# Loading the gated feed-forward's first operands during the last batch of lane attention

## The reference, cut to what matters

```python
x = x + tanh(g_xattn[1]) * L1_xattn(layernorm(x), ctx, ctx, ...)   # "lane attention"
x = x + tanh(g_ffn[1]) * L1_ffn(layernorm(x), gate_w, up_w, down_w, gate_a, ...)

def _L1_ffn_ref(x, gate_w, up_w, down_w, gate_a, gate_b, up_a, up_b, down_a, down_b):
    gate = _matmul_lora(x, gate_w, gate_a, gate_b)      # x @ w.T + (x @ a.T) @ b.T
    up = _matmul_lora(x, up_w, up_a, up_b)
    hidden = jax.nn.silu(gate) * up
    return _matmul_lora(hidden, down_w, down_a, down_b)
```

## Time and profile before

| what | us |
|---|---|
| median of 3 runs (lowest, highest) | 3406.77 (3404.89, 3408.68) |
| the profiled execution's own time | 3397.87 |
| its span, first to last instruction | 3396.2 |
| PE busy in the span | 3206.3 (94%) |
| last matmul of lane attention starts | 1878.14 |
| first matmul of the gated feed-forward starts | 1893.09 |
| its first product (L2329) starts | 1910.27 |

### The profile page before, as it was taken

How to read it: one execution, slowest core, us unless ns; L and a number is a source line. 1 busy time by engine, 2 the same in 40 slices (tenths; PEclk the granted TensorE clock), 3 DMA queues, 4 the chain that set the end, 5 groups by cost and what they waited for, 6 DMA issues and landing times. The chain is left out here.

```text
span 3396.2 us, 52096 instructions
## 1 busy us (share of the span) xinstructions
PE 3206.3 (94%) x20924; PEld 2468.6 (73%) x20924; DVE 1424.9 (42%) x2020; ACT 893.4 (26%) x1233; POOL 347.8 (10%) x304
## 2 busy tenths in 40 slices
PE   7999569998999989999999799999999999999999
PEld 4656437777788866666666688888888888778777
DVE  8888588882200028787777321222212122300000
ACT  3333343332211125555454211111111111200000
POOL 2000000000000013332232101111110100000000
PEclk9999779998999989999999799999999999999999
DMA  6776522212422231221221432222222222642443
GB/s 144 154 153 133 173 76 72 75 63 87 143 66 63 74 130 69 82 99 74 80 80 56 164 114 95 100 88 101 88 95 95 99 94 104 228 152 96 145 143 104
DMA packets 341895, 361.09 MB, mean 106 GB/s; under 512 B 154624, under 2 KB 261744, under 8 KB 339840
## 3 DMA queue, kind: packets, MB, share of 16 engines
q1 hardware_dynamic: 338304, 356.28, 33.2%
q10 hardware_dynamic: 3456, 2.90, 0.3%
HBM read 215.23 MB, written 135.36 MB: 103 GB/s over the span
## 5 line engine op out<-in xcount | busy, mean ns | idle before, releaser
L2329 PE MATMUL g_ps<-g_xs,g_wt 128*128 128x512 f32 x4128 | 948.9, 390 | 0.0
L2329 PEld LDWEIGHTS g_ps<-g_xs,g_wt 128*128 128x128 f32 x4128 | 774.7, 188 | 159.9
L2388 PE MATMUL g_ps<-g_wd,g_h 128*128 128x512 f32 x2016 | 460.5, 390 | 6.6 <-DVE g_act_out L2245 3.7
L2388 PEld LDWEIGHTS g_ps<-g_wd,g_h 128*128 128x128 f32 x2016 | 379.1, 188 | 87.2 <-DVE g_act_out L2245 4.2
L2245 DVE SCALAR_TENSOR_TENSOR g_act_out<-g_ps,g_g,g_act_out 128x512 f32<-128x512 f32 (+1 forms) x88 | 66.0, 751 | 672.8 <-ACT g_act_out L2178 672.8
L2178 ACT ACTIVATE g_act_out<-g_ps 128x512 f32<-128x512 f32 (+1 forms) x88 | 52.6, 598 | 634.5 <-PE g_ps L2329 634.4
L1336 PE MATMUL kv_gps<-kv_xh,kv_wh 128*128 128x512 f32 x512 | 202.1, 395 | 1.0 <-DVE kv_xl L1281 1.0
L1336 PE MATMUL kv_gps<-kv_xh,kv_wl 128*128 128x512 f32 x512 | 199.9, 390 | 0.0
L1336 PE MATMUL kv_gps<-kv_xl,kv_wh 128*128 128x512 f32 x512 | 199.7, 390 | 0.0
L1059 PE MATMUL f_gps<-f_xt,f_qwh 128*128 128x256 f32 x1024 | 192.1, 288 | 1.4 <-DVE f_xt L914 1.4
L2118 POOL TENSOR_TENSOR g_wt<-g_raw,g_wt 128x1024 fp32r<-128x1024 f32 x43 | 102.9, 2392 | 853.9 <-ACT g_wt L2155 853.9
(11 more groups left out here) (267 smaller groups left out, 4333.6 us busy)
## 6 DMA issues: line engine op xcount, KB each, us to landing
g_h<-g_hidden SPq DMA_DIRECT2D x176, 256.0 KB, 2.6
g_hidden<-g_h SPq DMA_DIRECT2D x84, 512.0 KB, 2.7
kv<-kv_y SPq DMA_DIRECT2D x16, 1024.0 KB, 5.7
g_down<-g_raw SPq DMA_DIRECT2D x22, 512.0 KB, 2.8
g_raw<-g_down SPq DMA_DIRECT2D x22, 512.0 KB, 4.2
g_raw<-in_L_ffn_gate_w_dram SPq DMA_DIRECT2D x21, 512.0 KB, 4.0
g_raw<-in_L_ffn_up_w_dram SPq DMA_DIRECT2D x21, 512.0 KB, 3.9
g_raw<-in_L_ffn_down_w_dram SPq DMA_DIRECT2D x21, 512.0 KB, 4.0
```

The costliest lines, as they stand in the source:

```text
L2329: w = pe.matmul(gps[:, c % 2, m, :], wt[m][i][:, l, ks], xs[c][:, r, k, :], start=(k == 0 and a == 0), stop=(k == NK - 1 and a == 2))
L2388: w = pe.matmul(to, tile[:, p % RING, l, cols], wd[f][:, r, os], start=(f == 0 and a == 0), stop=False)
```

## The change

Lane attention's last batch issues the feed-forward's first loads from SP's queue, behind the store of batch 14's result and ahead of `store_norm(14)`: the factors, the gate and up weights of block 0, the factors of blocks 0 and 1, and token tiles 0 and 1. For that the `early` tiles become views into one arena of fixed size, with feed-forward tiles at the places of attention tiles that are free by then (`kv` and `q` of batch 14, `x`); `la`, `lb` and `sl1` lie where both stages leave room. POOL clears `la`, `lb` and both `sl` tiles in batch 1 of lane attention. The scope of the `early` tiles now ends with the feed-forward. Token tiles 0 and 1 go to `xb` in place of `xa`, and the loads of tiles 2 to 13 that stay in the feed-forward are in a new order.

```diff
+    rows = at("x", 0, [P, 2, D])
+    raw = [at(f"wraw{i}", 8192 + 4096 * i, [P, D]) for i in range(2)]
+    factors = at("factors", 24576, [P, columns])
...
+             "graw": [at(f"graw{i}", offset, [P, D]) for i, offset in enumerate((16384, 20480, 4096))],
+             "gx": [at(f"gx{i}", offset, [P, D]) for i, offset in enumerate((24576, 0))],
+             "gh": at("gh", 8192, [P, 4, 2, 256], F32R),
+             "sl0": at("sl0", 24576 + 4096, [P, 3, P], F32R)}
...
+            def feed_forward():
+
+                sp.wait_ge(S["zero"], 4)
+                for rows, part, done in ((gate_a, early["la"][0:R3, :], "la"), (up_a, early["la"][UP:UP + R3, :], "la"),
+                                         (down_b, early["lb"][0:R3, :], "lb")):
+                    sp.dma_start(part.bitcast(F32), rows).then_inc(E[done], 16)
+                sp.wait_ge(S["t"], NK * (B - 1))
+                for m, w in enumerate((gate_wt, up_wt)):
+                    sp.dma_start(early["graw"][m][:, :].rearrange("p (k h) -> p k h", h=P),
+                                 w.rearrange("(k p) h -> p k h", p=P)[:, :, 0:P]).then_inc(E[f"graw{m}"], 16)
+                for part, first in ((early["sl0"], 0), (early["sl1"], P)):
+                    if first:
+                        sp.wait_ge(E["sl"], 48)
+                    for a, rows, m in ((gate_b, 0, 0), (up_b, UP, 1), (down_a, 0, 2)):
+                        sp.dma_start(part[rows:rows + R3, m, :].bitcast(F32), a[:, first:first + P]).then_inc(E["sl"], 16)
+                sp.wait_ge(S["ynout"], 32)
+                sp.dma_start(early["gx"][0][:, :], norm_out[0]).then_inc(E["gx0"], 16)
+                sp.wait_ge(S["xb"], B)
+                sp.dma_start(early["gx"][1][:, :], norm_out[1]).then_inc(E["gx1"], 16)
...
+                else:
+                    feed_forward()
                 store_norm(b - 1)
...
+                    if isinstance(b, int) and b == 1 and 3 <= c < 7:
+
+                        part = (early["la"][:, :], early["lb"][:, :], early["sl0"][:, :, :], early["sl1"][:, :, :])[c - 3]
+                        pool.memset(part.bitcast(F32), 0.0).then_inc(S["zero"], 1)
...
-            load_x(0)
-            load_x(1)
-            load_gate_up(0, 0)
-            sp.wait_ge(S["zero"], 4)
-            sp.dma_start(la[0:R3, :].bitcast(F32), gate_a).then_inc(S["consts"], 16)
-            sp.dma_start(la[UP:UP + R3, :].bitcast(F32), up_a).then_inc(S["consts"], 16)
-            load_factors(0, 0)
-            load_x(2)
-            load_x(3)
-            load_gate_up(0, 1)
-            sp.dma_start(lb[0:R3, :].bitcast(F32), down_b).then_inc(S["down_b"], 16)
+            for n in range(2, 6):
+                load_x(n)
             load_down(0)
-            for n in range(4, 8):
-                load_x(n)
-            load_factors(1, 1)
-            for n in range(8, 14):
+            for n in range(6, 14):
                 load_x(n)
...
-            pool.memset(la[:, :].bitcast(F32), 0.0).then_inc(S["zero"], 1)
-            pool.memset(lb[:, :].bitcast(F32), 0.0).then_inc(S["zero"], 1)
             pool.memset(ident[:, :], 0.0).then_inc(S["c1"], 1)
-            for i in range(2):
-                pool.memset(sl[i][:, :, :].bitcast(F32), 0.0).then_inc(S["zero"], 1)
```

More of the change, by code:

```diff
@@ L18 @@
 EPS = 1e-5
+PAST = 30336
 class Scope:
@@ L1355, in _, with lane_tiles, at, lane_attention @@
             products(NB - 1, 1)
-def lane_tiles(nc, ctx, columns):
+def lane_tiles(nc, ctx, columns, ranks):
     s = Scope(nc, ctx, "early")
[L1361 to L1364, removed]
-             "q": factors[:, 0:D].rearrange("p (k t) -> p k t", t=P),
-             "wo": [rows[:, 0, :], rows[:, 1, :], raw[0], raw[1]]}
-    sems = {n: s.sem(n) for n in "g ql k0 kvl wo0 wo1 wo2 wo3".split()}
+    base = -(-nc.sbuf_base // 32) * 32
+    s.sb("arena", [P, (PAST - (base - nc.sbuf_base)) // 4])
+    def at(name, offset, shape, dt=F32):
+        return nc.alloc_sbuf_tensor_at(f"early_{name}", shape, dt, offset=base + offset)
+    rows = at("x", 0, [P, 2, D])
+    raw = [at(f"wraw{i}", 8192 + 4096 * i, [P, D]) for i in range(2)]
+    factors = at("factors", 24576, [P, columns])
+    tiles = {"x": rows, "wraw": raw, "factors": factors, "kv": at("kv", 16384, [P, 2 * NK, P]), "g": at("g", PAST - 64, [P, 2]),
+             "q": factors[:, 0:D].rearrange("p (k t) -> p k t", t=P),
+             "wo": [rows[:, 0, :], rows[:, 1, :], raw[0], raw[1]],
+             "graw": [at(f"graw{i}", offset, [P, D]) for i, offset in enumerate((16384, 20480, 4096))],
+             "gx": [at(f"gx{i}", offset, [P, D]) for i, offset in enumerate((24576, 0))],
+             "gh": at("gh", 8192, [P, 4, 2, 256], F32R),
+             "sl0": at("sl0", 24576 + 4096, [P, 3, P], F32R)}
+    arena = -(-nc.sbuf_base // 32) * 32
+    over = arena - base
+    tiles["la"] = at("la", over + 4 * 2 * D * 20, [P, D], F32R)
+    tiles["lb"] = at("lb", over + 4 * 2 * D * 20 + 4096, [P, D], F32R)
+    tiles["sl1"] = at("sl1", over + 4 * 2 * D * 21, [P, 3, P], F32R)
+    tiles["free_to"] = arena + 4 * 2 * D * 20
+    sems = {n: s.sem(n) for n in "g ql k0 kvl wo0 wo1 wo2 wo3 graw0 graw1 gx0 gx1 la lb sl".split()}
     return tiles, sems
-def lane_attention(nc, early, E, q_in, kv_in, x_in, wot, bo, x_out, norm_out):
+def lane_attention(nc, early, E, q_in, kv_in, x_in, wot, bo, x_out, norm_out, gate_wt, up_wt, gate_a, up_a, gate_b, up_b,
+                   down_a, down_b):
     U = 8
@@ L1418, in lane_attention @@
         rs = s.sb("rs", [P, 2, U])
+        assert nc.sbuf_base <= early["free_to"]
+        R3, UP = gate_a.shape[0], 64
         ring = s.ps("ring", [P, 2, U, P])
@@ L1426, in lane_attention @@
         names = ("consts c1 um gate gbo wow wowl ones km s vt ov w mx sub ex t te pv pve ot rcp on oh ol vaf xl xb res "
-                 "out stats aggr rstd yn ynout").split()
+                 "out stats aggr rstd yn ynout zero").split()
         S = {n: s.sem(n) for n in names} | {"ql": E["ql"], "kvl": E["kvl"]}
@@ L1828, in _, with swiglu_ffn @@
             project(B - 1, (LAST + 1) % 2)
-def swiglu_ffn(nc, x_in, norm_in, gates, gate_wt, up_wt, down_wt, gate_a, up_a, gate_b, up_b, down_a, down_b, out):
+def swiglu_ffn(nc, early, E, x_in, norm_in, gates, gate_wt, up_wt, down_wt, gate_a, up_a, gate_b, up_b, down_a, down_b, out):
     HID = gate_wt.shape[1]
@@ L1856, in swiglu_ffn @@
         wt = [[at(f"wt{m}{i}", 16 + 2 * i + m, [P, 2, D]) for i in range(2)] for m in range(2)]
-        la = at("la", 20, [P, D])
-        lb = at("lb", 20.5, [P, D])
-        sl = [at(f"sl{i}", 21 + i * 0.1875, [P, 3, P]) for i in range(2)]
+        la, lb = early["la"], early["lb"]
+        sl = [early["sl0"], early["sl1"]]
         wd = [at(f"wd{f}", f, [P, 2, D]) for f in range(LAST)]
@@ L1865, in swiglu_ffn @@
         xa = nc.alloc_sbuf_tensor_at("g_xa", [P, 8, D], F32, offset=base + int(4 * SLOT * 12))
-        raw = [s.sb(f"raw{m}", [P, D]) for m in range(3)]
+        raw = early["graw"]
         act_out = s.sb("act_out", [P, 2, 512])
-        xb = [s.sb(f"xb{i}", [P, D]) for i in range(2)]
-        h = s.sb("h", [P, RING, 2, 256], F32R)
+        xb = early["gx"]
+        h = early["gh"]
         ident = s.sb("ident", [P, P])
@@ L1885, in swiglu_ffn @@
         down = nc.dram_tensor("g_down", (NF, P, D), F32, kind="Internal").ap()
-        names = ("consts down_b c1 gate zero zl xt xth xtl sld wp wa wh wl gu si hf hh hl dst "
+        names = ("consts c1 gate zl xt xth xtl wp wa wh wl gu si hf hh hl dst "
                  "wh2 wl2 pd res").split()
-        S = {n: s.sem(n) for n in names}
-        xld = [s.sem(f"xld{i}") for i in range(10)]
-        wld = [s.sem(f"wld{m}") for m in range(3)]
+        S = {n: s.sem(n) for n in names} | {"sld": E["sl"]}
+        xld = [s.sem(f"xld{i}") for i in range(8)] + [E["gx0"], E["gx1"]]
+        wld = [E["graw0"], E["graw1"], s.sem("wld2")]
         dld = [s.sem(f"dld{i}") for i in range(2)]
@@ L1929, in place @@
         def place(n):
-            if n < 12:
-                return xa[:, n % 8, :], xld[n % 8], 16 * (n // 8) + 16
-            return xb[n % 2][:, :], xld[8 + n % 2], 16 * (n // 14) + 16
+            if 2 <= n < 12:
+                return xa[:, (n - 2) % 8, :], xld[(n - 2) % 8], 16 * ((n - 2) // 8) + 16
+            return xb[n % 2][:, :], xld[8 + n % 2], 16 * (n // 12 + n // 14) + 16
         def turned(n):
@@ L1942, in load_x @@
                 to, done, _ = place(n)
-                if 8 <= n < 12:
+                if 10 <= n < 12:
                     sp.wait_ge(S["xt"], n - 7)
-                elif n >= 14:
-                    sp.wait_ge(S["xt"], n - 1)
+                elif n >= 12:
+                    sp.wait_ge(S["xt"], n - 11 if n < 14 else n - 1)
                 sp.dma_start(to, norm_in[n]).then_inc(done, 16)
             def load_factors(f, i):
-                if not isinstance(f, int) or f >= 2:
-                    wait_apart(sp, S["c1"], (S["sld"], 48 * f), (S["wp"], merged(f - 2, 2) + 1))
```

(12 more changed lines are left out.)

4 lines of the change are left out of this document (1 added, 3 removed).

## The result

The changed kernel takes **3413.03 us** (median of 12 runs, 3404.32 to 3415.44) against 3406.82 for the kernel before (12 runs, 3399.58 to 3410.34): a ratio of 1.0019, 95% interval 1.0011 to 1.0026, so 3.7 to 8.9 us slower. I had forecast 3401.5, with 3405.5 as the upper end. Its profiled execution took 3413.45, span 3411.8, mean granted clock 0.974.

A forecast was written before the change was run, and what follows sets the result against it. PE, busy 94% of the span, was taken as the bound, with time to be had where it idles or runs slowly. 6.3 us at the merge, less 0.5 at the end and 0.5 for the clock: 3406.77 - 5.3 = 3401.5; range 3397.0 to 3405.5.

The forecast's parts named there:

- The first product 6.3 us earlier: Feed-forward start: DVE adds the gate part at 1894.6, not 1900.90, so the first full product also comes 6.3 us early.
- The barrier's 0.5 us moved to the end: Second meeting, of the `early` scope, leaves the stage's start for the program's end: 0.5 us gained, 0.5 us lost.
- The clock: PE's clock falls after waits at the feed-forward's start; 0.5 us taken off for a longer first wait, 3 us either way.
- less kindly: Rival: one clock fall more, at the stage's last wait, leaving 2.4 us gained, 3404.4; chance 0.13.
- The loads of tiles 2 to 5 in time: Token loads left behind the barrier land before PE wants them, with 1.5 us of slack at the tightest.
- The early loads priced at nothing: SP's thirteen issues after batch 14's result finish at about 1862, 5.5 us before `store_norm(14)` is due; cost nothing.
- The memsets in POOL's waits: Four memsets in batch 1 of lane attention fit POOL's 1.99 us waits: cost nothing, under 3.8 us if uncovered.
- the stage from 4 to 7.5 us gained: Main forecast, from the feed-forward's earlier start: 3399.5 to 3403, chance 0.60, an eighth of it beyond 6.8 us.
- The 8.9 us between the profiled execution and the median: Timed median of the kernel before lay 8.9 us above its profiled execution; unexplained and taken to stay.
- the same row for row: After the gate merge the chain keeps its lengths: 6.90 us to the part of down, 9.37 to the first product.
- The rival "slower": Moved tiles or memsets slow DVE's 128 lane attention steps, 0.1 us each: 3414.3; chance 0.04.

The follow-up runs named there:

- e1: The changed kernel with its arena 32 B longer, so down weights and hidden tile start equal modulo 128 B: 3405.90 us, ratio 1.0003.
- e7: The changed kernel with an arena length that puts the down weights a multiple of 512 B from the hidden tile: 3399.33 us, ratio 0.9982.
- e8: e7 plus pads so lane attention's output tiles start at the same place modulo 512 B as the output weights: 3394.40 us, ratio 0.9970 to the kernel before.
- e12: The kernel before with `oh` and `ol` moved 224 B, to a distance from their weights that is a multiple of 256 B, not 512: 3399.85 us, ratio 0.9982.
- e3: The kernel before with hidden tile `h` 32 B further on and the two small tiles behind it 64 B: 3414.33 us, ratio 1.0029.
- e2: The kernel before with everything of the feed-forward 32 B further on, operand distance still 0: 3405.22 us, ratio 1.0001.
- e5: The kernel before with down weights `wd` 32 B and hidden tile `h` 64 B further on: 3415.72 us, ratio 1.0033.
- e9: The kernel before with hidden tile `h` moved by 256 B and the tiles behind it by 512 B: 3405.82 us, one execution.

## Why the prediction was wrong

- **The first product 6.3 us earlier: right.** Forecast from 1910.27 to 1904.0, relative to attention's end; measured 6.3. All three changed kernels profiled besides (e1, e7, e8) show 25.8 us again.
- **The barrier's 0.5 us moved to the end: right**, 0.4 measured.
- **The clock: mechanism right, size and place off.** I took 0.5 us for the longer wait ahead of the part of down (it grew from 2.56 to 4.49 us) and gave the rival "less kindly", one fall more at the last wait, 0.13. That fall came. Four lines of PE's timeline of the changed kernel, to compare with the earlier trace rows:

```profile
1933.38 1.44 PE L2330 MATMUL g_ps<-g_ident,g_xa 128*128 128x128 f32 x8 [3.28 <-DVE g_xs L2247]
1934.47 4.32 PE L2359 MATMUL g_ps<-g_xs,g_wt 128*128 128x512 f32 x12
...
1953.04 1.06 PE L2330 MATMUL g_ps<-g_ident,early_gx 128*128 128x128 f32 x8 [2.49 <-DVE g_xs L2247]
1953.86 4.58 PE L2359 MATMUL g_ps<-g_xs,g_wt 128*128 128x512 f32 x12
```

  Behind the wait of 2.49 the turn is still at full speed, then the twelve matmuls take 4.58 in place of 2.99; before, the wait of 2.46 had cost nothing. The fall after 3.28 was milder (4.32 against 5.02), the product at 1906.44 longer (4.67 against 3.51). In sum the column products took 1.9 us more than before, where I had put 0.5. In the other three changed kernels they took 1.5 to 2.1 more, and 985.7 to 986.1 in all in seven of the eight kernels with the old start (987.3 in e12). The granted clock in those stretches, to compare with the earlier trace rows, confirms the level of 1.2 GHz for part of each (0.50 all through the stage's first turns):

```profile
1953.00:1958.00 5.00, 4.96 (x19) 4.14 (x20) 1.23 (x1) 1.01 (x1) 0.15 (x1) 0.66 0.95 311
1933.00:1939.00 6.00, 5.62 (x24) 4.78 (x25) 1.46 (x2) 1.01 (x1) 0.50 (x1) 0.72 0.01 3
1906.00:1911.00 5.00, 5.00 (x17) 4.01 (x16) 1.64 (x2) 1.11 (x2) 1.27 (x1) 0.60 1.05 381
1891.00:1896.00 5.00, 4.88 (x24) 4.88 (x24) 1.35 (x2) 2.02 (x2) 0.07 (x1) 0.50 0.71 243
```

- **The loads of tiles 2 to 5 in time: right.** PE's turn at 1896.20 waited for nothing. The loads of `g_xa`, ten where there were twelve:

```profile
DMA to landing us min/median/max: 4.2/8.4/10.3
```

- **The early loads priced at nothing: right in effect, off in size.** This whole trace runs 2.8 us later here (the store of batch 14's result goes out at 1852.86, not 1850.08), so SP's last early issue is to be counted from that store: 12.8 us behind it, where 11.9 was forecast, and 4.7 us ahead of `store_norm(14)` in place of 5.5. The cover was enough. The memsets in POOL's waits cost nothing either; they shortened the waits by 0.9 us (the second large one) and 0.4 (the small ones). The row reads `early_kv` and so belongs to batch 2, but three of batch 1's own waits had the same length, 1.98 to 2.00.
- **Small slips that moved nothing:** of the stage from 4 to 7.5 us gained, a fifth lies beyond 6.8, not an eighth (the 0.12 is that fifth of 0.60). The 8.9 us between the profiled execution and the median, which I took to stay, did not: in the changed kernel they are 0.4. In part they were a milder clock in the profiled execution of before, 0.974 where the median of the others is 0.972, with only 3.4 us of its down phase at the lower level, as little as in any of the twelve profiles.
- **The step that failed** is the one I took without a word: that behind the first product everything keeps its speed. The words "the same row for row" reach only to that product, at 1904.0, and the sum carried the rest of the feed-forward, 1500 us, over unchanged, although the change gives 1968 matmuls of it other addresses relative to each other. It was a term put at nothing, and it was worth +12.9 us, twice the gain: a pitch of 233.4 ns in place of 226.8, which e3 shows without the early loads and e7 takes away with them in place. The rival "slower" did say that tiles have moved in memory, and its 3414.3 is near the 3413.0 measured. That is chance: it placed the cost in DVE's steps of lane attention, which kept their length. I had asked which engine might be slowed by a move, and only in the stage where the loads were added.

SBUF — State Buffer of the Trainium skill, section "Operand start alignment", asks that an operand start at a multiple of its element size and says of itself that this is about legality, not speed. Every start here obeys it, at a pitch of 233.4 ns as at 226.8.

## What to carry to other kernels

When a change moves tiles, look through the whole rest of the program for products that read them, and compare the start of the loaded operand with that of the streamed one before and after: a sub-percent gain at a stage boundary is easily outweighed by 3% on 2000 matmuls. In this kernel a pad that makes the distance a multiple of 256 B was worth about three times the change at one place (13.5 us against 4.2, at an equal clock) and as much as the change at the other (4.6). Before a difference of a few us is given to a cause, compare the granted clocks of the executions. In a profile, a busy engine without gaps and with fewer instructions in an equal stretch at an equal clock is this sign; the share of busy time hides it.

## What was not expected of the hardware

- The pitch of f32r matmuls with 512 streamed columns at a granted clock of 1.00 depended on the distance of the two operands' starts in a partition, modulo 256 B: 226.7 to 227.4 ns at 0, 232.3 or 232.4 at 128, 233.2 to 233.4 at 32, 64 and 160. Their absolute starts did not matter (e2, e5). Why, no run shows; within the tiles the operands' steps are multiples of 512 B, which fits a pattern that stays the same over a whole tile.
- The down phase's profiled length scattered by up to 8 us among kernels with the same pitch (492.8 before, 500.3 in e9). The profile of before was the shortest of them; this is most of the 8.9 us by which it lay below the timed median, which I could not explain from the trace alone.
